# Value products of two key tiles in a row, a fourth probability slot, and row maxima turned as one square

## What is computed

```
def _L0_xattn_ref(query, key, value, wq, bq, wk, bk, wv, bv):    # 16 heads of 16
    q = (query @ wq.T + bq).reshape(B, L, H, Dh).transpose(0, 2, 1, 3)
    ...
    attn = jax.nn.softmax(jnp.einsum('bhld,bhsd->bhls', q, k) / scale, axis=-1)
    out = jnp.einsum('bhls,bhsd->bhld', attn, v)
...
def _L0_ffn_ref(src, ...):
    # self-attention with rotary positions, the same 16 heads, out projection Wo
    x = _rmsnorm(src + sa, norm1_w)
    shared = _swiglu(flat @ W_shared_in) @ W_shared_out
    # router: one of 2 groups, 2 of its 4 experts, weights w
    h = _swiglu(flat @ W1_shared)
    for e in range(E):
        routed = routed + h @ W2_experts[e] * w[:, e:e + 1]
    return _rmsnorm(x + (shared + routed).reshape(Bb, Tt, C), norm2_w)

x = x + jnp.tanh(g_xattn[0]) * _L0_xattn_ref(_layernorm(x), ctx_1024, ctx_1024, ...)
x = x + jnp.tanh(g_ffn[0]) * _L0_ffn_ref(_layernorm(x), ...)
```

## Time and profile before

| | us |
|---|---|
| median of 3 runs | 798.07 |
| lowest, highest run | 795.81, 799.25 |
| the profiled execution | 799.23 |
| its span in the trace | 797.5 |
| mean granted TensorE clock, as a share of full speed | 0.983 |

### The profile page before, as it was taken

How to read it: one execution, slowest core, us unless ns; L and a number is a source line. 1 busy time by engine, 2 the same in 40 slices (tenths; PEclk the granted TensorE clock), 3 DMA queues, 4 the chain that set the end, 5 groups by cost and what they waited for, 6 DMA issues and landing times.

```text
span 797.5 us, 10572 instructions
## 1 busy us (share of the span) xinstructions
PE 752.8 (94%) x3606; PEld 347.6 (44%) x3606; DVE 512.8 (64%) x776; ACT 417.4 (52%) x766; POOL 225.2 (28%) x342
## 2 busy tenths in 40 slices
PE   5889999999999999999999999999999899989994
PEld 3432343343233233233423423426645755458883
DVE  2598848847868868878797798743366022523664
ACT  3447868877758767776675777683211122222000
POOL 3451123223315405304222410010105612400654
PEclk9989999999999999999999999999999999999998
DMA  8882233226124414413411331006003824000010
GB/s 244 222 240 62 59 106 121 80 51 200 47 57 164 108 41 136 129 41 94 144 42 41 125 105 52 1 2 210 1 0 134 274 100 132 0 0 1 34 40 34
DMA packets 51316, 73.32 MB, mean 92 GB/s; under 512 B 6976, under 2 KB 42304, under 8 KB 51264
## 3 DMA queue, kind: packets, MB, share of 16 engines
q1 hardware_dynamic: 47248, 63.80, 27.0%
q0 software_dynamic: 2816, 8.46, 2.8%
q10 hardware_dynamic: 1200, 0.40, 0.2%
HBM read 45.04 MB, written 27.33 MB: 91 GB/s over the span
## 4 chain that ended last, share of the span: by engine, by line
PE 75%; DVE 13%; ACT 6%; issue 3%; DMA 1%; POOL 1%; ACTq 1%; DVEq 0%; POOLq 0%
PE ps L1479 35%; PE ps L1627 11%; PE ps L1651 11%; PE ps L1599 10%; DVE negm L1135 7%; ACT hS L891 3%; PE ps L1474 2%; DVE bst L1013 2%; PE ps L1615 1%; PE ps L1607 1%; PE ps L1538 1%; DMA bv_bc<-in_L_xattn_bv_dram 1%; ACT rows L797 1%; PE ps L1533 1%; PE ps L1559 0%
## 5 line engine op out<-in xcount | busy, mean ns | idle before, releaser
L1135 DVE TENSOR_REDUCE negm<-ps 128x2 f32<-128x1024 f32 x256 | 304.9, 1223 | 80.4 <-PE ps L1599 73.3
L891 ACT ACTIVATE hS<-ps 128x512 f32<-128x512 f32 x512 | 278.5, 600 | 106.4 <-PE ps L1651 104.5
L1651 PE MATMUL ps<-w 98*128 98x512 bf16 x512 | 168.0, 386 | 5.9 <-ACT hS L891 3.3
L1599 PE MATMUL ps<-w 96*128 96x512 bf16 x512 | 154.6, 383 | 5.5 <-DVE negm L1135 4.9
L1627 PE MATMUL ps<-hS,mix 128*17 128x512 f32 x1024 | 134.7, 598 | 0.2
L1651 PEld LDWEIGHTS ps<-w 98*128 98x128 bf16 x512 | 42.5, 97 | 153.4 <-ACT hS L891 70.6
L1599 PEld LDWEIGHTS ps<-w 96*128 96x128 bf16 x512 | 49.0, 99 | 58.6 <-DVE negm L1135 11.5
L1331 DVE SCALAR_TENSOR_TENSOR ctxs<-qk,ps 128x512 f32<-128x512 f32 x32 | 22.0, 688 | 76.6 <-ACT qk L925 76.0
L925 ACT ACTIVATE qk<-ps 128x512 f32<-128x512 f32 x32 | 19.1, 597 | 82.5 <-PE ps L1479 78.6
L1479 PE MATMUL ps<-w,hS 128*128 x256 | 57.4, 387 | 2.0 <-issue 2.0
L1479 PEld LDWEIGHTS ps<-w,hS 128*128 128x128 f32 x256 | 49.7, 195 | 9.9 <-issue 2.8
(11 more groups left out here) (209 smaller groups left out, 891.6 us busy)
## 6 DMA issues: line engine op xcount, KB each, us to landing
w<-scrq SPq DMA_DIRECT2D x32, 384.0 KB, 4.1
scrk<-mix SPq DMA_DIRECT2D x24, 256.0 KB, 2.1
scrq<-mix SPq DMA_DIRECT2D x16, 384.0 KB, 3.3
scrq<-mix SPq DMA_DIRECT2D x24, 256.0 KB, 2.5
w<-scrk SPq DMA_DIRECT2D x32, 192.0 KB, 3.0
w<-scrk SPq DMA_DIRECT2D x32, 128.0 KB, 3.0
w<-in_L_ffn_W_experts_dram SPq DMA_DIRECT2D x8, 512.0 KB, 8.0
mix<-scrf SPq DMA_DIRECT2D x4, 528.0 KB, 5.6
```

Source lines behind the costliest of these rows:

```text
L891: nc.scalar.activation(prob[:, kt % PROB_SLOTS, s % HG, :], slot_bank(("unit", u)), ACT.Exp, scale=SC).then_inc(s_exp, 1)
L1135: V.tensor_reduce(negm[:, gi % 2, 2 * t2:2 * t2 + 2, h], ps[:, bank:bank + 2, :], AX.X, ALU.max, negate=True).then_inc(s_re, 1)
L1599: last = MM(ps[:, bank + t, :], qs[0:STK, g, h, tt * P:(tt + 1) * P], ks[0:STK, g, h, :], start=True, stop=True)
L1651: MM(take(("unit", u)), ks[:, g, h, kt * P:(kt + 1) * P], qs[:, g, h, :], start=True, stop=True).then_inc(s_sT, 1)
```

## The change

- `values` is called twice in a row at steps 3 and 11, and not at 7 and 15. At step 3 come key tiles 2 and 3 of the group before, at step 11 key tiles 0 and 1 of this group. After the last group, tiles 2 and 3 follow each other.
- There are four probability slots. The fourth lies in `fin[:, 1]`, so that weight is loaded later: after the last values, ahead of the experts' weights. The PE waits for it (`s_wr`) before the first "routed" product.
- The maxima are laid out as head by tile (`negm`), both parts side by side in 32 columns of a 128x128 square `m2` whose rest is zero. PE turns the square in one transposition instead of four of 8 columns, ACT copies 32x128 instead of 8x512, and one DMA instead of two carries the rows into the stack: 32 pieces of 256 bytes instead of 8 of 1,024. DVE clears `m2` once at the start.

```diff
-PROB_SLOTS = 3
+PROB_SLOTS = 4
...
-        prob = hS[:, 0:12].rearrange("p t c j -> p (t c j)").rearrange("p (s h l) -> p s h l", s=PROB_SLOTS, h=HG)
+        prob = [hS[:, 4 * i:4 * i + 4].rearrange("p t c j -> p (t c j)").rearrange("p (h l) -> p h l", h=HG) for i in range(3)]
+        prob.append(fin[:, 1].rearrange("p c n -> p (c n)").rearrange("p (h l) -> p h l", h=HG))
...
-        negm = sb("negm", [P, 2, TT, HG], F32)
-        m2 = sb("m2", [P, 2, TT, MPART, HG], BF16)
-        mTs = sb("mTs", [MPART * HG, 2, L], BF16)
+        negm = sb("negm", [P, 2, HG, TT], F32)
+        m2 = sb("m2", [P, 2, P], BF16)
+        mTs = sb("mTs", [MROWS, 2, P], BF16)
...
-                (fin[:, 1], f_w1.rearrange("(k p) n -> p k n", p=P)),
...
+            sp.wait_ge(s_pv, NI * KTS)
+            sp.dma_start(fin[:, 1], f_w1.rearrange("(k p) n -> p k n", p=P)).then_inc(s_wr, 16)
             sp.wait_ge(s_sT, NI * UNITS)
...
-                nc.scalar.activation(mTs[:, gi % 2, :], slot_bank(("turned", gi))[:, 0:L // 2].bitcast(BF16)[0:MPART * HG, :],
+                nc.scalar.activation(mTs[:, gi % 2, :], slot_bank(("turned", gi))[:, 0:P // 2].bitcast(BF16)[0:MROWS, :],
...
-                for t in range(MPART):
-                    act.dma_start(qs[STK + t:STK + t + 1, gi % NG, :, :],
-                                  mTs[t * HG:(t + 1) * HG, gi % 2, :]).then_inc(s_mrow, 16)
+                act.dma_start(qs[STK:KROWS, gi % NG, :, :], mTs[:, gi % 2, :]).then_inc(s_mrow, 16)
...
+            V.memset(m2[:], 0.0).then_inc(s_ini, 1)
...
-                    m, o = negm[:, gi % 2], m2[:, gi % 2]
-                    link(V.tensor_copy(o[:, :, 0, :], m))
-                    mark(V.tensor_tensor(o[:, :, 1, :], m, o[:, :, 0, :], ALU.subtract))
+                    m = negm[:, gi % 2].rearrange("p h t -> p (h t)")
+                    o = m2[:, gi % 2, 0:MROWS].rearrange("p (s r) -> p s r", s=MPART)
+                    link(V.tensor_copy(o[:, 0], m))
+                    mark(V.tensor_tensor(o[:, 1], m, o[:, 0], ALU.subtract))
...
-                o = take(("turned", gi))[:, 0:L // 2].bitcast(BF16)
-                for tt in range(TT):
-                    last = TR(o[0:MPART * HG, tt * P:(tt + 1) * P],
-                              m2[:, gi % 2, tt].rearrange("p s h -> p (s h)"), identb[:])
+                o = take(("turned", gi))[:, 0:P // 2].bitcast(BF16)
+                last = TR(o, m2[:, gi % 2, :], identb[:])
...
-                        if h == HG - 1 and (kt or gi):
-                            values(*((gi, kt - 1) if kt else (gi - 1, TT - 1)))
+                        if s in (HG - 1, 3 * HG - 1) and (kt or gi):
+                            for t in (2 * (kt // 2) + 2, 2 * (kt // 2) + 3):
+                                values(*((gi, t - TT) if kt > 1 else (gi - 1, t)))
...
-            values(GROUPS - 1, TT - 1)
+            for t in (TT - 2, TT - 1):
+                values(GROUPS - 1, t)
...
+                    if at[0] == 0 and at[1] == 0:
+                        pe.wait_ge(s_wr, 16)
...
-N_BIAS, N_SMALL, N_LARGE, N_LATE = 5, 5, 10, 3
+N_BIAS, N_SMALL, N_LARGE, N_LATE = 5, 5, 10, 2
```

More of the change, by code:

```diff
@@ L65, in flamingo_block @@
     VM = DH + 1
+    MROWS = MPART * HG * TT
     assert (B, L, D, DH, CT, TT, DC, EPG) == (4, 512, 256, 16, 2, 4, 64, 4)
@@ L343, in flamingo_block @@
         s_wl = sem("ffn_weights_loaded")
+        s_wr = sem("routed_weights_loaded")
         s_w2 = sem("expert_weights_loaded")
@@ L560, in _ @@
             load_x(3)
-            sp.wait_ge(s_mrow, 16 * MPART)
+            sp.wait_ge(s_mrow, 16)
             stack(1)
@@ L780, in max_turned @@
                 act.wait_ge(s_mtf, gi + 1)
-                ge(act, s_mrow, (gi - 1) * 16 * MPART)
-                nc.scalar.activation(mTs[:, gi % 2, :], slot_bank(("turned", gi))[:, 0:L // 2].bitcast(BF16)[0:MPART * HG, :],
+                ge(act, s_mrow, (gi - 1) * 16)
+                nc.scalar.activation(mTs[:, gi % 2, :], slot_bank(("turned", gi))[:, 0:P // 2].bitcast(BF16)[0:MROWS, :],
                                      ACT.Copy).then_inc(s_mts, 1)
@@ L890, in _ @@
                             act.wait_ge(s_pv, kt - PROB_SLOTS + 1)
-                        nc.scalar.activation(prob[:, kt % PROB_SLOTS, s % HG, :], slot_bank(("unit", u)),
+                        nc.scalar.activation(prob[kt % PROB_SLOTS][:, s % HG, :], slot_bank(("unit", u)),
                                              ACT.Exp, scale=SC).then_inc(s_exp, 1)
@@ L1005, in setup @@
                                       raw.rearrange("p (h j f) -> p f j h", f=2, j=DH // 2)[:, f]).then_inc(s_ini, 1)
-                dve.wait_ge(s_ini, 4 + EPG + 1 + 6)
+                dve.wait_ge(s_ini, 5 + EPG + 1 + 6)
                 dve.sem_inc(s_set, 1)
@@ L1134, in row_max @@
                 dve.wait_ge(s_rf, c + 1)
-                V.tensor_reduce(negm[:, gi % 2, 2 * t2:2 * t2 + 2, h], ps[:, bank:bank + 2, :], AX.X, ALU.max,
+                V.tensor_reduce(negm[:, gi % 2, h, 2 * t2:2 * t2 + 2], ps[:, bank:bank + 2, :], AX.X, ALU.max,
                                 negate=True).then_inc(s_re, 1)
@@ L1138, in row_max @@
                     dve.wait_ge(s_re, c + 1)
-                    m, o = negm[:, gi % 2], m2[:, gi % 2]
-                    link(V.tensor_copy(o[:, :, 0, :], m))
-                    mark(V.tensor_tensor(o[:, :, 1, :], m, o[:, :, 0, :], ALU.subtract))
+                    if gi == 0:
+                        dve.wait_ge(s_ini, 5 + EPG)
+                    m = negm[:, gi % 2].rearrange("p h t -> p (h t)")
+                    o = m2[:, gi % 2, 0:MROWS].rearrange("p (s r) -> p s r", s=MPART)
+                    link(V.tensor_copy(o[:, 0], m))
+                    mark(V.tensor_tensor(o[:, 1], m, o[:, 0], ALU.subtract))
                     ready(s_m2)
@@ L1626, in values @@
                 for h in range(HG):
-                    last = MM(ps[32 * h:32 * h + VM, 6, :], vp[n % 2][:, kt, g * HG + h, :], prob[:, kk % PROB_SLOTS, h, :],
+                    last = MM(ps[32 * h:32 * h + VM, 6, :], vp[n % 2][:, kt, g * HG + h, :], prob[kk % PROB_SLOTS][:, h, :],
                               start=(kt == 0), stop=(kt == TT - 1))
@@ L1641, in _ @@
             pe.wait_ge(s_one, 2)
-            pe.wait_ge(s_ini, 4 + EPG)
+            pe.wait_ge(s_ini, 5 + EPG)
             for n in range(NI):
@@ L1649, in _ @@
                         if s == 0:
-                            pe.wait_ge(s_mrow, (gi + 1) * 16 * MPART)
+                            pe.wait_ge(s_mrow, (gi + 1) * 16)
                         MM(take(("unit", u)), ks[:, g, h, kt * P:(kt + 1) * P], qs[:, g, h, :],
```

## The result

The changed kernel takes 828.35 us (median of 4 runs, 826.38 to 837.35), the kernel before 798.66 us beside it (795.81 to 800.14). The ratio over all runs is 1.040, with a 95% interval of 1.034 to 1.046 (that of the two medians is 1.037; one run of the changed kernel was 9 us slower than the other three). The direction and a part of the mechanism were forecast, the size was not: 820 was predicted. The median lies 1.65 us inside the upper end of the range, 830. The ratio, put on the 798.07 from which the prediction started, gives 830.1, just past it. The profiled execution took 828.2 us, 29.0 more than that of the kernel before.

A forecast was written before the change was run, and what follows sets the result against it. PE bounds the kernel before; after the change, waits on DVE's reductions through the two-deep ring cost 12.0 + 7.1 + 0 + 1.5 + 2 + 1 = 23.6 us, taken as 22: 798.07 + 22 = 820, range 800 to 830.

The forecast's parts named there:

- PE's saving: Two value products in a row take PE 1.84 us, saving 0.2 per double call, 13 us of PE work.
- What DVE then allows: Pairs wait for DVE's reductions: half without heads costs 5.98 us for 5.64, half with heads 7.33 for 6.5.
- The handoff: PE may write a score item 0.15 to 0.18 us after DVE is done with the one two before it.
- The square: nothing: One maxima turn for four, hidden by DVE's chain, costed at nothing; without that cover, a gain of at most 9 us.
- The moved load, the slots: Weight load behind the last values has 95 us of cover, cost 0; four probability slots cause no wait.
- ACT isn't later than DVE here: In the half without heads, four exp take 2.06 us from 0.43 on, so ACT adds no delay.
- I take 0 for the 24 together: The 24 halves with projection tiles between pairs cost 0 in sum, with ends of -10 and +8 us.
- 1.5 for the statistics: Row statistics of 1.40 us on DVE behind step 14's pair now delay the fourth pair: 2 x 0.75 us.
- 2 for the cross attentions' values: DVE's addition at step 2 for cross attentions 2 and 3 waits for the doubled value product: +0.9 each, 2 us.
- PE stays the bound: Rival: DVE keeps up, PE's 13 us and 3 to 9 of turns come off, 776 to 782 us; chance 0.10.
- The second product starts anew: Rival: the second value call costs 1.06 us for 0.86, adding 12 us: 832 us; chance 0.08.
- the rows come late: Rival: the maxima's DMA from step 11 lands too late for step 0, 31 us if it took 5: 851; chance 0.02.

The follow-up runs named there:

- singles: Changed kernel with value products back as single calls at steps 3, 7, 11 and 15, square of maxima, slots and moved load kept: 789.77 us.
- half reductions: Row maxima taken over 256 of 512 keys: 800.44 us in the changed kernel, 778.28 us with single value products and the square.
- half exp: Exp on 256 of 512 queries, here with maxima over 256 of 512 keys too: changed kernel 777.99 us, with single value products 768.70 us.
- the statistics moved: Changed kernel with row statistics of cross attentions 2 and 3 moved from step 14 of the second group to step 4 of the third: 832.82 us.

## Why the prediction was right in kind and short in size

- **"PE's saving", 0.2 us per twin: right.** A twin measured 1.85 us (1.84 predicted), and with DVE and ACT relieved the half without heads fell by 0.22.
- **"What DVE then allows", 5.98 and 7.33 us: right.** Measured 5.86 and 7.15 in the group shown. The handoff was too long in the working: the earlier trace rows give 0.20 and 0.15, where I wrote 0.15 to 0.18, and the group shows 0.11 to 0.13.
- **"The square: nothing": right under twins** (2.6 us less the clock), and worth 5.8 to 7.2 with singles, inside the 3 to 9 that the prediction gave if the cover were gone.
- **The moved load, the slots: right,** 0.
- **"ACT isn't later than DVE here": wrong.** It was true of the clean half that I worked out. But ACT runs dry behind a twin just as DVE does, and has the copy of bank 6 behind it. With half reductions twins lost 22.2 us, and 9.3 with half exp too: 13 of the 22 were ACT's.
- **"I take 0 for the 24 together": this is the step that failed.** I cut the trace from one turn of heads to the next, before and after. The 14 intervals without projection tiles grew by 13.4 us less the clock, where the sum had 14 x (0.8 + 0.34) = 16.0 and 1.5 for the statistics; many of them already held a wait or a statistic before. The 15 with tiles grew by 10.0 less the clock, each of them by something. The sum had 5.1 for them: 3.1 for such of their halves as I had counted free of tiles, 2 for the cross attentions' values, and 0 for the halves with a tile, reasoning that a tile does for DVE what the value product did. None gained. (By the hooks 17 halves without heads are free of tiles, and not 21, so the sum had 1.4 too much there.) The last two intervals grew by 2.2, where 1 was taken. Together 25.6, against 23.6, of which I took 22: that the total of the waits came so near is luck, two errors of 4 to 5 us that nearly cancel.
- **Not in the sum at all, put at nothing without a reason:** the clock's falls, +5.1 in the stage and -3.3 in the end stage in this run, and 1.4 ahead of the first heads. 25.6 + 5.1 - 3.3 + 1.4 = 28.8 of the 29.0 measured. Of the 7 us between these 29 and my 22, 3.6 are waits (the tiles' stretches alone were 4.9 short) and 3.2 are the clock and the start. Runs differ in this: three of the four had a mean clock of 0.984 and took 826.4 to 828.5, the one of 837.35 had 0.968.
- **The rivals.** "PE stays the bound" is refuted by the time and the waits. The rule that the Trainium skill states, in "TensorEngine Tiling (Array Packing)", Key Properties, that a change of tiling mode drains the engine, agrees with the twin's price, 1.85 for two calls; it says nothing of what the drained engine's neighbours need. "The second product starts anew" and "the rows come late" are refuted (1.85; the square gains). What stays open is why the clock falls where it does, and what holds PE in the stretches with tiles once both engines are relieved.

## What to carry to other kernels

Before bunching the work of the engine that bounds a kernel, count how long the others can live on what is buffered: here two pairs for DVE (2.36 us, and at least one of them under way) and three score tiles for ACT (1.6 us) stood against a bunch of 1.84 us, and an evenly spread piece of PE work was what kept both fed. DVE, at 77% of busy time behind a two-deep buffer, had no room here for a gap of a microsecond; compare period and latency step by step, not shares. When a change has several parts, run each alone: the one that was nearly free to write, the square of maxima, is worth 7 us, and the one it came with cost 39. With one more step, maxima over half of the keys, the singles run at 778.28 us; softmax is the same for any shift, but that version trusts that no score of the other half exceeds the shift by so much that exp overflows.

## What the runs showed of the hardware

- Idle gaps can cost twice. Gaps of 1.3 and 1.6 us on TensorE were followed by several us at the lower clock (granted 0.62 over 9 us, 0.72 over 6), 3.4 and 1.7 us more by the estimate above. Not every gap is: of those of 1.3 us or more in the attention stage, two of seven in the change and five of five with the statistics moved. Across the runs the clock took 0 us from the nine stages in which PE's longest gap was 1.00 us or less, and 5 to 22 us from the five others. A change that adds waits should be budgeted with that on top.
- The small bf16 cast of the maxima on DVE, 0.17 us, took 1.61 to 2.16 where GpSimd was at a 128x1024 tensor, and ended with it:

```profile
309.15 2.13 POOL L636 TENSOR_TENSOR qk<-qk,mix 128x1024 f32<-128x1024 f32 x1 [1.64 <-ACT mix L811]
309.71 1.61 DVE L1140 CAST m<-negm 128x16 bf16<-128x16 f32 x1
```

  (the kernel before; 309.71 + 1.61 = 311.32, 309.15 + 2.13 = 311.28). It happened in 4 groups, and there it cost nothing. In the change the same 1.6 us stood on the path, in the half with heads.
